# Half-contraction attention products for the first two tiles, with reordered loads and row sums, in an adaLN kernel on one core

## The reference

```
mod = (_silu(L0_c) @ L0_wmod).reshape(L0_c.shape[0], 6, 1, -1)
sa, ca, ga, sb, cb, gb = (mod[:, 0], mod[:, 1], mod[:, 2], mod[:, 3], mod[:, 4], mod[:, 5])
h = _layernorm(x, axis=-1) * (1 + ca) + sa
x = x + ga * _L0_attn_ref(h, L0_attn_mask, L0_attn_weight, L0_attn_bias)
h = _layernorm(x, axis=-1) * (1 + cb) + sb
x = x + gb * _L0_ffn_ref(h, ...)       # silu(h @ gate.T) * (h @ up.T), then @ down.T

# in _L0_attn_ref: a 32x32 block of the weight counts where its mask has a sum over 0
wb = weight.reshape(Nb, BH, Kb, BW) * bm[:, None, :, None].astype(weight.dtype)
out = jnp.einsum('bsk,nk->bsn', data, w) + bias
```

## Time and profile before

| | us |
|---|---|
| median of 3 runs | 1124.59 (1124.07 to 1126.71) |
| the profiled execution | 1126.06 |
| its span, first to last instruction | 1124.3 |
| PE busy in it | 1089.5 (97%) |
| DVE busy | 739.7 (66%) |
| ACT busy | 428.7 (38%) |
| POOL busy | 375.0 (33%) |

### The profile page before, as it was taken

The page is one execution under the profiler, slowest core; times in us unless marked ns, Lnnn a source line. Parts: engine busy times, 40 slices in busy tenths (PEclk is TensorE's granted clock), DMA queues, the critical chain, the costliest instruction groups (busy, mean ns, idle before and its releaser), DMA issues. The chain is left out here.

```text
span 1124.3 us, 13245 instructions
## 1 busy us (share of the span) xinstructions
PE 1089.5 (97%) x4741; PEld 509.9 (45%) x4741; DVE 739.7 (66%) x926; ACT 428.7 (38%) x783; POOL 375.0 (33%) x346
## 2 busy tenths in 40 slices
PE   4899999999999999999999999999999899999998
PEld 1544454555444444444444444444444344444444
DVE  2739367767678898888797888879545343334434
ACT  1332236656556455445555555555432000000000
POOL 1105237546655353315655564655200000000000
PEclk8699999999999999999999999999999999999999
DMA  9993212426353555446666665675288665565431
GB/s 342 404 387 83 75 40 73 113 57 203 125 197 103 166 173 177 116 126 195 183 206 192 188 180 175 194 198 178 76 345 333 235 245 230 218 245 220 184 144 38
DMA packets 130001, 206.94 MB, mean 184 GB/s; under 512 B 20624, under 2 KB 99216, under 8 KB 127504
## 3 DMA queue, kind: packets, MB, share of 16 engines
q1 hardware_dynamic: 124640, 184.08, 49.8%
q0 software_dynamic: 5296, 22.02, 5.5%
HBM read 137.39 MB, written 68.68 MB: 183 GB/s over the span
## 5 line engine op out<-in xcount | busy, mean ns | idle before, releaser
L1302 PE MATMUL pA<-work 128*128 128x512 f16 x1680 | 377.0, 379 | 4.6 <-ACT work L1043 2.9
L1302 PEld LDWEIGHTS pA<-work 128*128 128x128 f16 x1680 | 163.7, 98 | 205.1 <-ACT work L1043 6.0
L1166 PE MATMUL pA<-work 128*128 128x512 f32 x512 | 225.0, 593 | 0.0
L1302 PE MATMUL pB<-work 128*128 128x512 f16 x752 | 175.9, 379 | 1.4 <-DVE work L1700 1.4
L1166 PEld LDWEIGHTS pA<-work 128*128 128x128 f32 x512 | 95.0, 190 | 112.3 <-issue 111.4
L1722 DVE SCALAR_TENSOR_TENSOR work<-work 128x512 f16<-128x512 f16 x144 | 122.8, 875 | 19.2 <-ACT work L1063 19.0
L1369 PE MATMUL pA<-work 128*128 128x512 f16 x600 | 134.4, 379 | 0.0
L913 ACT ACTIVATE work<-pB,small 128x128 f32<-128x128 f32 x256 | 92.6, 477 | 72.2 <-PE pB L1155 60.9
L1043 ACT ACTIVATE work<-pA 128x512 f32<-128x512 f32 x126 | 74.6, 592 | 116.4 <-PE pA L1302 111.2
L1302 PEld LDWEIGHTS pB<-work 128*128 128x128 f16 x752 | 73.5, 98 | 90.1 <-DVE work L1700 2.1
L1369 PE MATMUL pB<-work 128*128 128x512 f16 x480 | 109.0, 383 | 3.3 <-DMA work<-h_left_scratch 3.3
(11 more groups left out here) (170 smaller groups left out, 1067.7 us busy)
## 6 DMA issues: line engine op xcount, KB each, us to landing
work<-h_scratch SPq DMA_DIRECT2D x8, 4480.0 KB, 13.7
h_scratch<-work SPq DMA_DIRECT2D x60, 512.0 KB, 3.1
work<-in_L_wmod SPq DMA_DIRECT2D x10, 2048.0 KB, 16.2
work<-in_L_ffn_gate_w SPq DMA_DIRECT2D x84, 128.0 KB, 3.3
work<-in_L_ffn_up_w SPq DMA_DIRECT2D x84, 128.0 KB, 2.9
work<-down_scratch SPq DMA_DIRECT2D x7, 1280.0 KB, 11.5
work<-in_L_ffn_down_w SPq DMA_DIRECT2D x68, 128.0 KB, 2.8
work<-in_L_attn_data SPq DMA_DIRECT2D x16, 512.0 KB, 4.4
```

The source lines that it names most:

```text
L1166: last = pe.matmul(pA[:, 2 * par(t) + h, :], hT1[par(t)][:, c, :], wT[:, c, h * H:(h + 1) * H], start=(c == 0), stop=(c == KT - 1))
L1302: last = pe.matmul(ps, w[:, m, c], bc[b][:, mv_, s, c], start=begin, stop=(i == n - 1 and c == KT // 2 - 1 and s == 1), skip_group_check=True)
```

## The change

A tile's contraction has eight pieces of 128. Pieces 0 to 3 of it need only the first halves of shift and scale, which are modulation pieces 0 and 2. The change runs `attend(0, 0)` and `attend(1, 0)` in two halves: contraction 0 to 3 after the modulation pieces 0 and 2, contraction 4 to 7 after pieces 1 and 3.

- SP loads x tile 0, masks 0 to 3, piece 0, weights 0 to 3, piece 2, x tile 1, piece 1, piece 3, masks 4 to 7, weights 4 to 7, and goes on as before.
- PE sums rows in the order 0, 2, 1, 3 (`SUM_ORDER`). `columns_of_piece(m)` makes four columns from one piece, in place of eight from two. `transpose_half_of_second` turns tile 1 in two halves. `row_sum(4)`, `row_sum(5)`, `transpose(0, 2)` and `gate_row(2)` are put in another order.
- ACT copies the columns out in halves (`columns_out`) and shifts and scales in halves (`turn_out_half`, four activations each, for the tiles 0 and 1).
- DVE normalises tile 1 after the first masked weights and its four moves; POOL's step for tile 1 goes behind its first masked weight.

```diff
@@ sync
+            load_x(0)
+            load_masks(0)
+            load_piece(0)
+            load_weights(0)
+            load_piece(2)
+            load_x(1)
+            load_piece(1)
+            load_piece(3)
+            load_masks(1)
+            load_weights(1)
             load_piece(4)
@@ scalar
-            for m in range(4):
-                copy_row(m)
-            act.wait_ge(acc_used, 2)
...
+            def columns_out(half):
+                act.wait_ge(acc_used, half + 1)
+                c = slice(4 * half, 4 * half + 4)
+                act.activation(colm[:, 0:KT][:, c], colp[:, 0:KT][:, c], ACT.Copy).then_inc(cols1_ready, 1)
+                act.activation(colm[:, KT:2 * KT][:, c], colp[:, KT:2 * KT][:, c], ACT.Copy, bias=1.0).then_inc(cols1_ready, 1)
+                act.wait_ge(cols1_ready, 2 * half + 2)
...
+            copy_row(0)
             for u in range(4, KT):
                 move_row_half(u)
-            turn_out(1)
+            copy_row(2)
+            columns_out(0)
+            turn_out_half(0, 0)
+            turn_out_half(1, 0)
+            copy_row(1)
+            copy_row(3)
+            columns_out(1)
+            turn_out_half(0, 1)
+            turn_out_half(1, 1)
@@ tensor
+            row_sum(2)
+            columns_of_piece(2)
+            attend(0, 0, range(4))
+            transpose_half_of_second(0)
+            row_sum(1)
+            attend(1, 0, range(4))
+            columns_of_piece(1)
+            row_sum(3)
+            columns_of_piece(3)
+            attend(0, 0, range(4, KT))
+            transpose_half_of_second(1)
             mask_total_of(1)
-            attend(0, 0, range(3, KT))
+            attend(1, 0, range(4, 6))
             turn_rows(4)
...
+            attend(0, 1)
             row_sum(4)
+            transpose(0, 2)
+            attend(1, 1, range(4))
             row_sum(5)
-            attend(0, 1, range(4, KT))
+            attend(1, 1, range(4, KT))
             gate_row(2, rowp[0])
-            transpose(0, 2)
-            attend(1, 1)
@@ vector
             norm1(0)
-            norm1(1)
             mask_rows_of(0)
...
+            norm1(1)
             mask_rows_of(1)
```

More of the change, by code:

```diff
@@ L322, in adaln_kernel @@
         hT1_ready = sem("hT1_ready")
+        z1_half_turned = sem("z1_half_turned")
+        hT1_half_ready = sem("hT1_half_ready")
         x_copied = sem("x_copied")
@@ L373, in adaln_kernel, with sums_until @@
         last_stored = sem("last_stored")
+        SUM_ORDER = [0, 2, 1, 3, 4, 5, 6, 7, 8, 9]
+        def sums_until(m):
+            return SUM_ORDER.index(m) + 1
         TURNS = [0, 2, 1, 3, 4, 6, 5, 7]
@@ L548, in load_piece @@
                 elif m >= 4:
-                    sp.wait_ge(row_summed, 5 if m == 9 else m - 3)
+                    sp.wait_ge(row_summed, sums_until(4 if m == 9 else m - 4))
                 dst = mp[m].rearrange("p (t n) -> p t n", t=KT)
@@ L756, in _ @@
             pool.tensor_copy(xg[0], xt[0]).then_inc(x_copied, 1)
-            rstd_of(0, 1)
-            pool.tensor_copy(xg[1], xt[1]).then_inc(x_copied, 1)
             for n in range(2, KT, 4):
@@ L763, in _ @@
                 mask_rows(pool, TURNS[n], masked_by_pool)
+                if n == 2:
+                    rstd_of(0, 1)
+                    pool.tensor_copy(xg[1], xt[1]).then_inc(x_copied, 1)
             def sums(r):
@@ L902, in copy_row, with shift_scale @@
                 act.activation(dst, src, ACT.Copy).then_inc(row_copied, 1)
-            for m in range(4):
-                copy_row(m)
-            act.wait_ge(acc_used, 2)
[L907 to L912, removed]
+            def columns_out(half):
[4 more added lines that the diff above has]
+                act.wait_ge(cols1_ready, 2 * half + 2)
+            def shift_scale(dst, src, L, cs=range(KT)):
+                for c in cs:
                     last = act.activation(dst[:, c, :], src[:, c, :], ACT.Identity,
@@ L930, in evacuate, with turn_out_half @@
                    .then_inc(evacuated, 1)
-            turn_out(0)
+            def turn_out_half(t, half):
+                if half == 0 and t == 1:
+                    act.wait_ge(z1_half_turned, 1)
+                else:
+                    act.wait_ge(t_done[0], t + 1)
+                done = hT1_ready if half else hT1_half_ready
+                shift_scale(hT1[t], z1T_c, 0, range(4 * half, 4 * half + 4)).then_inc(done, 1)
             def move_row_half(u):
@@ L1156, in transpose, with transpose_half_of_second @@
                 last.then_inc(t_done[L], 1)
+            def transpose_half_of_second(half):
+                zc = z1.rearrange("p (c k) -> p c k", c=KT)
+                pe.wait_ge(z_done[0], 2)
+                pe.wait_ge(hT1_ready if half else hT1_half_ready, 1)
+                for c in range(4):
+                    last = pe.transpose(z1T[:, half, c * P:(c + 1) * P], zc[:, 4 * half + c], ident)
+                last.then_inc(t_done[0] if half else z1_half_turned, 1)
             def attend(t, h, ks=range(KT)):
-                if h == 0 and ks[0] == 0:
+                if h == 0 and t < 2:
+                    pe.wait_ge(hT1_half_ready if ks[0] < 4 else hT1_ready, t + 1)
+                elif h == 0 and ks[0] == 0:
                     pe.wait_ge(hT1_ready, t + 1)
@@ L1169, in attend, with columns_of_piece @@
                     last.then_inc(attn_done, 1)
+            def columns_of_piece(m):
+                v, half = m // 2, m % 2
+                pe.wait_ge(row_copied, sums_until(m))
+                if half:
+                    pe.wait_ge(cols1_ready, 2)
+                for c in range(4 * half, 4 * half + 4):
+                    last = pe.matmul(colp[:, KT * v + c:KT * v + c + 1], acc[v][:, P * c:P * (c + 1)], share,
+                                     start=True, stop=True)
+                if v == 1:
+                    last.then_inc(acc_used, 1)
             def columns(v, dst):
@@ L1226, in _ @@
             pe.wait_ge(silu_c_done, 1)
[L1227 to L1230, removed]
             mask_total_of(0)
-            for n in range(4):
+            row_sum(0)
+            turn_rows(0)
+            pe.wait_ge(row_copied, 1)
+            for n in range(1, 4):
                 turn_rows(n)
-            transpose(0, 1)
+            columns_of_piece(0)
             pe.wait_ge(wT_by_dve, 4)
             pe.wait_ge(wT_ready, 4)
-            attend(0, 0, range(0, 3))
+            row_sum(2)
[9 more added lines that the diff above has]
+            transpose_half_of_second(1)
             mask_total_of(1)
-            attend(0, 0, range(3, KT))
+            attend(1, 0, range(4, 6))
             turn_rows(4)
[L1241 to L1244, removed]
+            attend(1, 0, range(6, 7))
+            turn_rows(5)
+            attend(1, 0, range(7, 8))
+            turn_rows(6)
+            turn_rows(7)
             pe.wait_ge(wT_ready, 2 * KT - 4)
             pe.wait_ge(mask_bits, 2)
-            pe.wait_ge(cols1_ready, 2)
-            attend(0, 1, range(4))
+            pe.wait_ge(cols1_ready, 4)
+            attend(0, 1)
             row_sum(4)
+            transpose(0, 2)
+            attend(1, 1, range(4))
             row_sum(5)
-            attend(0, 1, range(4, KT))
+            attend(1, 1, range(4, KT))
             gate_row(2, rowp[0])
-            transpose(0, 2)
-            attend(1, 1)
             for t in range(2, NT + 1):
```

13 lines of the change are left out of this document (4 added, 9 removed).

## The result

The changed kernel takes 1127.72 us in the median of 20 runs (1125.70 to 1129.42), against 1124.66 for the kernel before (20 runs, 1122.61 to 1127.41). The ratio is 1.0026, with a 95% interval of 1.0019 to 1.0033: slower by 3.1 us. That is just under the 3.4 us (0.3%) that the prediction called measurable, but 1.000 lies outside the interval. The profiled execution took 1127.24 us, with a span of 1125.4.

A forecast was written before the change was run, and what follows sets the result against it. PE was taken as the bound, with idle time and half clock only near the start. +1.9 at X and +1.3 behind it gave +3.2: 1129.3 from the profiled execution, 1127.8 from the median, middle 1128.5; range 1122 to 1132.5.

The forecast's parts named there:

- X: Moment PE reaches `attend(0, 1)`, the second column half of tile 0: 66.72 us before, forecast 68.6, later by 1.9.
- What bounds the kernel: PE busy in nearly every slice but the first two; only there is its granted clock low.
- Loads: Start of the queue: masks 0 to 3 in at 12.2 us, piece 0 at 17.5, piece 2 at 28.2.
- Until the first product: Start to first half product: 34.3 us at full clock, 39.1 at half; 37.0 taken, against 49.25 before.
- rival (a): Full clock from 17.5 us on: first half product at 34.3, X = 62.9; 1123.5 or 1122.1 us; chance 0.26.
- From there to X: First half product to `attend(0, 1)`: 28.6 us at full clock, 4.85 of it idle, plus 3.0 lost to low clock.
- Behind X: After `attend(0, 1)` begins: the later gate row delays DVE's normalising of tile 3; PE loses 1.3 us, nothing more.
- the stall: Before tile 3 is turned, PE waits 1.3 us for DVE, where before there was 6.4 us of slack.
- rival (d): DVE's lateness of 7.7 us is not absorbed at tile 4; PE stalls 2 to 4 us more: 1131.5; chance 0.05.
- (c): Loads share the engines; piece 0 or weights 0 to 3 land 2 us later than by order: 1130.5; chance 0.05.
- (b): Half clock throughout: first half product at 39.1, X = 71.7; 1132.4 and 1130.9, middle 1131.7 us; chance 0.21.
- The transposes and the clock: Skill's rule that transposes do not count as PE activity would leave the clock at half, 1131.7; the trace disagreed.

## Why the prediction was right or wrong

The time was forecast as 1128.5 in a range of 1122 to 1132.5, and is 1127.72. It was on the side of slower, and near to it in size: +3.1 by the medians against +3.2 in the sum. But the sum comes out for partly other reasons, and that the total agrees is in part luck: the sum had +1.9 at X and +1.3 behind it, and measured were some +0.2 at X, +1.6 behind it, and the rest in a fall of the clock that it did not have.

- **What bounds the kernel**: right. The differences found are PE's idle time or PE's clock, but for the 0.4 of the finer order. That only the first two slices have low clock was the page's rounding: the earlier trace rows hide a fall near 890 us in the trace of before, and the second trace of the same kernel had one at 149 us.
- **Loads**: the order was right, the forecast times were 1 us too late. Row sum 0 started at 16.48 in place of 17.5 and waited for its piece. The times came from the first trace of the kernel before, whose pieces had landed 1.1 us later than in its second.
- **Until the first product**: the term failed. 37.0 was taken, between 34.3 and 39.1, and 32.81 is below both. The 1.5 us under the full-clock bound are the loads and DVE's moves behind them (from 23.34 in place of 24.9). The other 2.7, to the 37.0, are the clock: PE ran at full from 24.16 at the latest (16 transposes in 2.36, row sum 2 in 1.92), so rival (a) was right up to here. I had taken the state of the like stretch before, where PE idled for more of the time.
- **From there to X**: 28.6 at full clock, and 3.0 lost. Measured 32.72, of which the two half products lost 1.64 and 1.41, 3.05 in all. The 1.87, 1.87, 1.37 and 0.84 of waiting stand against 1.9, 1.9, 1.6 and 0.65. The remaining 1.1 over the sum is 0.4 in the products (eight instructions take 3.54 before the next group starts, where the sum had 3.45), 0.3 in the waits (the mask total, 0.39, did not lie under the wait of 1.37 but ahead of it), and 0.2 each in the row sums and the turned rows. X was forecast at 68.6 and came at 65.5.
- **Against what X was set**: 66.72 was one trace. In two others of the kernel with an untouched start X was 64.97 and 64.44 (62.72 and four instructions, the kernel with the columns apart), so 65.4 in the mean of three. In the four traces with the changed start it was 65.53, 65.67, 66.10 and 64.97, 65.6 in the mean. The change moves X by some +0.2, not by -1.2, and not by +1.9. (From PE's first instruction, which begins at 9.3 to 10.1 us in these traces, the means are 55.5 and 55.8.) The traces of one kernel differ by more than that, so X is shown to be about the same, and no more. The prediction had noted that the profiled execution was 1.5 over the median, and took the middle for it; the late X, with its late loads, is a part of this.
- **Behind X**: the stall was forecast as 1.3 and is 1.20, and DVE's 7.96 are 7.97. The 0.4 of the finer order was not in the sum. Nothing later was late, so rival (d) falls; (c) falls by the loads, and (b) by the clock until 32.7.
- **The transposes and the clock**: between 20.05 and 26.4 us PE ran nothing but turned blocks, with one wait of 0.97, and row sum 2 behind them took 1.92, its length at full clock. The rule of the Trainium skill that the prediction weighed ("TensorE: Matmul & The Clock Gate", "Part 4: PE-mode transpose") would have the clock fall there; as a strict rule it does not hold in this trace either.

So: +0.2 at X, +0.4 and +1.2 behind it make 1.8 us of the 3.1. The order behind X was undone by itself and took 1.8 back (2.95 in its own set), 1.65 of it in this stretch of the trace. For the other 1.3 the fall of the clock at 149 us is the likely place: it took 3.3 us in both traces of the changed kernel, and 0 and 1.7 in those of the kernel before, and no run of the changed kernel has a mean granted clock without such a loss behind the start. Taking the columns apart took 2.8 back there and 0.9 in the kernel before. How the change brings it about is not shown.

## What to carry to other kernels

Work that is moved ahead, into a time in which TensorE waits for loads, gains only as much as the new waits leave over: a half product whose operand comes through a chain of row sum, copy, columns, copy and activations waits for that chain twice. Such a wait cost twice here, by its length and by the half clock of the product behind it; start the product at its first piece, and if PE has nothing else to do, let it do something useless. Before a sum in microseconds is made against one trace of a kernel whose start is not steady, look at a second one: here the first had its loads 1.1 us and X 1.75 us later than the second.

## What was not expected of the hardware

- The clock fell behind rather short pauses: a copy wait of 0.71, eight instructions of one column in 1.05 and a wait of 1.87, 3.6 us in all, lie ahead of the fall in both traces of the changed kernel. With a wait of 0.82 in place of 1.87 it fell in one trace and not in another (half products of 5.21 and 3.70). At 149 us PE was busy by the profile without a gap. In the changed kernel the clock fell there 2.3 us into the 32 instructions of one column (at 148.8, granted clock 0.89 in the stretch from 148 to 149), in the second trace of the kernel before only at 148.9, behind all 32 and the eight transposes after them, which ran from 144.16 to 148.7. With two pieces of a product between them it did not fall in any of the five traces.
- Ten useless instructions of 256 columns per wait, 2.7 us of PE's time that was idle else, kept the clock at full in both places of the changed kernel's trace, and the kernel got 7.0 us faster by the median. Added work made the kernel faster. In the kernel before, useless products between the row sums did not keep it: it fell twice before the first product.
- The profiled execution can be the slowest of a kernel's runs: 1125.78 against a median of 1120.73 for the kernel with useless products.
- The granted clock in the profile's rows begins at 1.00 and shows no half clock before the first fall, but row sum 0 of the changed kernel took 3.64 us, and row sum 2 took 1.92. The length of the instructions says that PE began at half clock, so in the first 20 us the clock is to be read from them.
